# Slot-ordered scratch for the keys and queries of a cross attention, loads behind the row of maxima, and batch 1's keys in the score loop

## What is computed

```python
x = _layernorm(x + _L0_attn_ref(x, ...))
def _L0_xattn_ref(x, cross_input, ...):
    q, k, v = x @ Wq + bq, x @ Wk + bk, x @ Wv + bv          # split in 16 heads
    y = softmax(q k^T * scale, causal) v
    qc, kc, vc = x @ Wcq + bcq, cross_input @ Wck + bck, cross_input @ Wcv + bcv
    y = y + softmax(qc kc^T * scale) vc                       # 256 queries x 1601 keys
    return y @ Wp + bp
x = _layernorm(x + _L0_xattn_ref(x, ctx_512, ...))
```

## Time and profile before

| | before |
|---|---|
| median of 3 runs | 784.41 us |
| lowest and highest | 782.75, 788.08 us |
| profiled execution, device time | 783.82 us |
| its span (first to last instruction) | 781.7 us |
| PE, DVE, ACT, POOL busy | 639.9, 521.7, 428.6, 175.6 us |
| bytes moved by DMA | 62.51 MB in 33067 packets |
| mean granted clock of PE | 0.904 |

### The profile page before, as it was taken

How to read it: one execution, slowest core, us unless ns; L and a number is a source line. 1 busy time by engine, 2 the same in 40 slices (tenths; PEclk the granted TensorE clock), 3 DMA queues, 4 the chain that set the end, 5 groups by cost and what they waited for, 6 DMA issues and landing times. The chain is left out here.

```text
span 781.7 us, 13389 instructions
## 1 busy us (share of the span) xinstructions
PE 639.9 (82%) x5152; PEld 350.8 (45%) x5152; DVE 521.7 (67%) x683; ACT 428.6 (55%) x774; POOL 175.6 (22%) x204
## 2 busy tenths in 40 slices
PE   7988589899999999999968769997304789887996
PEld 5654233333333333333323347883101466655884
DVE  4356979698999999999333458994587444526442
ACT  3555178688888888888860125555630212234223
POOL 6225344246760000000004120000240280004100
PEclk9999779899999999999995669999856879999999
DMA  7045656654341111110020057440000300000000
GB/s 187 1 138 200 196 164 206 208 172 132 105 123 52 49 49 50 49 49 3 4 74 24 1 202 309 140 134 0 0 0 0 149 0 1 1 0 1 1 0 28
DMA packets 33067, 62.51 MB, mean 80 GB/s; under 512 B 6968, under 2 KB 23360, under 8 KB 32496
## 3 DMA queue, kind: packets, MB, share of 16 engines
q1 hardware_dynamic: 26960, 31.84, 13.0%
q0 software_dynamic: 5440, 27.61, 10.2%
q10 hardware_dynamic: 608, 2.25, 1.3%
HBM read 41.46 MB, written 19.77 MB: 78 GB/s over the span
## 5 line engine op out<-in xcount | busy, mean ns | idle before, releaser
L853 ACT ACTIVATE prob<-ps 128x512 f32<-128x512 f32 (+2 forms) x480 | 252.5, 582 | 60.5 <-PE ps L676 53.9
L975 DVE TENSOR_REDUCE pm<-ps 128x2 f32<-128x1024 f32 x192 | 226.2, 1220 | 17.2 <-PE ps L638 15.3
L676 PE MATMUL ps<-qq,kc 50*128 50x256 bf16 (+1 forms) x832 | 136.7, 279 | 8.0 <-DMA qq<-mrow 7.9
L699 PE MATMUL ps<-prob,vst 128*9 128x256 f32 (+1 forms) x1664 | 130.1, 385 | 9.5 <-ACT o_all L841 9.5
L638 PE MATMUL ps<-kc,qq 48*128 48x512 bf16 x384 | 119.9, 401 | 4.8 <-DVE pm L975 3.5
L676 PEld LDWEIGHTS ps<-qq,kc 50*128 50x128 bf16 (+1 forms) x832 | 53.0, 96 | 103.6 <-ACT prob L853 72.7
L1097 POOL TENSOR_TENSOR y<-y 128x256 f32<-128x256 f32 x16 | 11.4, 722 | 193.5 <-issue 178.9
L699 PEld LDWEIGHTS ps<-prob,vst 128*9 128x9 f32 (+1 forms) x1664 | 25.1, 88 | 51.4 <-ACT prob L853 37.7
L982 DVE TENSOR_REDUCE nm<-ps 128x4 f32<-128x512 f32 (+1 forms) x32 | 30.6, 958 | 14.6 <-PE ps L626 14.5
L1778 ACT ACTIVATE prob<-s 128x512 f32<-128x512 f32 (+1 forms) x28 | 15.5, 567 | 45.3 <-PE s L1716 45.3
L638 PEld LDWEIGHTS ps<-kc,qq 48*128 48x128 bf16 x384 | 33.6, 95 | 13.6 <-DVE pm L975 8.9
(11 more groups left out here) (348 smaller groups left out, 1287.1 us busy)
## 6 DMA issues: line engine op xcount, KB each, us to landing
kc<-kc_scr SPq DMA_DIRECT2D x32, 150.1 KB
comb_bc<-comb_scr SPq DMA_DIRECT2D x8, 512.0 KB, 4.6
ctx<-ctx_scr POOLq DMA_DIRECT2D x1, 3204.0 KB, 16.0
kc<-kc_scr SPq DMA_DIRECT2D x32, 100.1 KB
raw<-in_wexp POOLq DMA_DIRECT2D x8, 384.0 KB, 7.8
exp_scr<-raw_high POOLq DMA_DIRECT2D x8, 384.0 KB, 3.5
exp_scr<-raw_low POOLq DMA_DIRECT2D x8, 384.0 KB, 7.0
up_high<-exp_scr SPq DMA_DIRECT2D x8, 256.0 KB, 2.8
```

The source lines that it names most:

```text
L676: last = pe.matmul(bank[0:p, j * TQ:(j + 1) * TQ], kc[s][rows, j, t * 128:t * 128 + p], qq[s][rows, 0, j, :], start=(j == 0), stop=True, s ...
L699: last = pe.matmul(o_ps[32 * hh:32 * hh + VW, kind * TQ + q0:(kind + 1) * TQ], value[:, hh * VW:(hh + 1) * VW], prob[0:k, (NST * n + t) % ...
L853: act.activation(prob[0:p, g % P_RING, 2 * e:2 * e + 2, q0:TQ], s2[0:p, k % S2_RING, 0:2 * w].rearrange("p (i q) -> p i q", i=2), ACT.Exp, ...
L975: dve.tensor_reduce(pm[:, m % 2, c, :, jt], banks, AX.X, ALU.max).then_inc(s1_read, 1)
```

## The change

It has five parts. (a) `kc_scr` and the three other scratches are laid out in slot order, [batch, 64 channels, 6 rows, 2 heads, columns], so that the 48 rows of a head pair lie together; every part is written in as many copies as the slot has: 6 writes for a batch of context keys instead of 3 (twice the bytes), and 6 for each kind of query or own key instead of 3 (the same bytes). (b) A unit is loaded with 2 transfers for the context keys instead of 6, so 8 instead of 12. (c) Batch 0's context keys are written by SP in three slabs (pieces 0, 1, and 2 with 3) as their parts become ready, instead of by POOL at the end; the cast of the masks on POOL comes after piece 1. (d) SP loads unit 1 ahead of the first row of maxima, and then unit m + 2 behind the row of unit m (before: units 1 and 2 ahead, unit m + 3 behind). (e) Batch 1's four key pieces and three value tiles, which stood ahead of the halves, move among the 22 halves; `late_keys` and `late_values` say which half each follows: keys at halves 0 to 7 and 13 to 16, values at 1, 3, 5, 7, 8 to 12, 14, and 16 to 20. The clearing of `o_ps` on DVE moves with them.

```diff
+PART_AT = (1, 2, 0)
-        kc_scr = nc.dram_tensor("kc_scr", [3, NB, 128, TK], BF16).ap()
-        xs_scr = {n: nc.dram_tensor(f"{n}_scr", [NB, 6, 128, TQ], BF16).ap() for n in ("ks", "qs", "qc")}
+        kc_scr = nc.dram_tensor("kc_scr", [NB, 64, 6, 2, TK], BF16).ap()
+        xs_scr = {n: nc.dram_tensor(f"{n}_scr", [NB, 64, 6, 2, TQ], BF16).ap() for n in ("ks", "qs", "qc")}
...
+            FIRST_SLABS = ((0, 0, 512), (1, 512, 512), (3, 1024, TK - 1024))
+            KEYS_OUT = ((first_out, 96 * len(FIRST_SLABS)), (j_out[1], 96), (j_out[0], 96), (j_out[1], 192))
...
-            FIRST_X, SECOND_X, SECOND_KEYS, LATE_KEYS = 4, 7, 10, 14
+            FIRST_X, SECOND_X, LATE_KEYS = 4, 7, 10
...
-            LATE_VALUES = DVE_VALUES + 3
+            late_keys = dict(zip([*range(8), *range(13, 17)], range(LATE_KEYS, len(pieces))))
+            late_values = dict(zip([1, 3, 5, 7, *range(8, 13), 14, *range(16, 21)], range(DVE_VALUES, len(values_order))))
...
                         for e in range(2):
-                            at, row = GROUP * e, 32 * g + 16 * e
-                            for part, r0, copies in ((0, 0, 3), (1, 3, 2), (2, 5, 1)):
-                                src = kc_scr[part, b, row:row + 16, :].rearrange("(c j) t -> c (j t)", j=2)
-                                sp.dma_start(kc[s][at + HD * r0:at + HD * (r0 + copies)],
-                                             src.unsqueeze(0).to_broadcast([copies, HD, 2 * TK])).then_inc(slot_in[s], 16)
+                            row = 16 * g + HD * e
+                            sp.dma_start(kc[s][head_rows(e)], kc_scr[b, row:row + HD].rearrange(
+                                "c r j t -> (c r) (j t)")).then_inc(slot_in[s], 16)
...
-                        if kind == "ks":
-                            for part, r0, copies in ((0, 0, 3), (1, 3, 2), (2, 5, 1)):
...
+                        for r in range(6):
+                            src = xk[:, KPART[r], q] if kind == "ks" else xq[:, PART_AT[QPART[r]], ("qc", "qs").index(kind), q]
+                            sp.dma_start(xs_scr[kind][b, :, r], src).then_inc(x_out[kind][b], 16)
...
-                            src = xs_scr[kind][b, :, row:row + 16, :].rearrange("r (c j) t -> r c (j t)", j=2)
+                            src = xs_scr[kind][b, row:row + HD].rearrange("c r j t -> (c r) (j t)")
...
+                    for j, c0, w in FIRST_SLABS:
+                        for ready, part in (((j_hi, j + 1), hi), ((j_mid, j + 1), mid), (lows(j), low)):
+                            sp.wait_ge(*ready)
+                            for r in range(6):
+                                if (hi, mid, low)[KPART[r]] is part:
+                                    sp.dma_start(kc_scr[0, :, r, :, c0:c0 + w], part[:, 0, c0:c0 + w]).then_inc(first_out, 16)
...
-                    for m in (1, 2):
-                        load_context(m)
+                    def load_unit(n):
+                        if n % NG == 0:
+                            sp.wait_ge(*KEYS_OUT[n // NG])
+                        if n >= SLOTS:
+                            sp.wait_ge(av_done, NST * (n - SLOTS + 1))
+                        load_context(n)
                         for kind in X_KINDS:
-                            load_split(kind, m)
+                            load_split(kind, n)
+
+                    load_unit(1)
                     for m in range(NU):
                         max_rows(m)
-                        n = m + SLOTS - 1
-                        if m < 3:
+                        if m < NB - 1:
                             for kind in X_KINDS:
                                 split_out(kind, m + 1)
-                        if n < NU:
...
+                        if m + 2 < NU:
+                            load_unit(m + 2)
...
-                        for part, src in enumerate((hi, mid, low)):
-                            pool.dma_start(kc_scr[part, b], src[:, b % 2, :]).then_inc(j_out[b % 2], 16)
+                        for r in range(6):
+                            src = (hi, mid, low)[KPART[r]]
+                            pool.dma_start(kc_scr[b, :, r], src[:, b % 2, :]).then_inc(j_out[b % 2], 16)
...
-                        if j in last_piece and is_ctx[j]:
+                        if j in last_piece[1:] and is_ctx[j]:
...
                     for h in range(HALVES + S1_LEAD):
                         half(h)
-                        if LATE_KEYS + h < len(pieces):
-                            keys(LATE_KEYS + h)
-                        if LATE_VALUES + h < len(values_order):
-                            values(LATE_VALUES + h)
+                        if h in late_keys:
+                            keys(late_keys[h])
+                        if h in late_values:
+                            values(late_values[h])
```

More of the change, by code:

```diff
@@ L271, in parts_of @@
                     return [xk[:, part, c0:c0 + w] for part in range(3)]
-                return [xq[:, part, ("qc", "qs").index(kind), c0:c0 + w] for part in (1, 2, 0)]
+                return [xq[:, part, ("qc", "qs").index(kind), c0:c0 + w] for part in PART_AT]
             def wait_parts_left(engine, j):
                 if is_ctx[j] and groups[pieces[j][0]][1] >= 2:
-                    engine.wait_ge(j_out[groups[pieces[j][0]][1] % 2], 16 * 3)
+                    engine.wait_ge(*KEYS_OUT[groups[pieces[j][0]][1] - 2])
             def low_on_dve(j):
@@ L360, in load_split @@
                         if g == 0:
[L361 removed]
+                            sp.wait_ge(x_out[kind][b], 16 * 6)
                         for e in range(2):
[L363 to L365 removed]
+                            row = 16 * g + HD * e
+                            dst = ks[s][head_rows(e)] if kind == "ks" else qq[s][head_rows(e), ("qc", "qs").index(kind)]
+                            src = xs_scr[kind][b, row:row + HD].rearrange("c r j t -> (c r) (j t)")
                             sp.dma_start(dst, src).then_inc(slot_in[s] if kind == "qc" else self_in[s], 16)
@@ L453, in _ @@
                         pool.dma_start(later[n][:], a[n]).then_inc(later_in, 16)
-                    for s in range(2):
-                        pool.wait_ge(j_out[s], 16 * 6)
+                    for b in range(NB):
+                        pool.wait_ge(*KEYS_OUT[b])
                     pool.wait_ge(v_act, len(values_order) - DVE_VALUES)
@@ L616, in _ @@
                         values(5 + i)
-                    for i in range(4):
-                        keys(SECOND_KEYS + i)
-                        if i < 3:
-                            values(DVE_VALUES + i)
                     def add_mask(o, mask, e):
@@ L823, in _ @@
                     high(4)
-                    for j in range(5, SECOND_KEYS):
+                    for j in range(5, LATE_KEYS):
                         middle(j - 1)
                         high(j)
-                    for i in range(4):
-                        middle(SECOND_KEYS + i - 1)
-                        high(SECOND_KEYS + i)
-                        if i < 3:
-                            values(DVE_VALUES + i)
-                    for i in range(len(values_order) - LATE_VALUES):
-                        if LATE_KEYS + i <= len(pieces):
-                            middle(LATE_KEYS + i - 1)
-                        if LATE_KEYS + i < len(pieces):
-                            high(LATE_KEYS + i)
-                        values(LATE_VALUES + i)
+                    for h in range(HALVES + S1_LEAD):
+                        if h == 0:
+                            middle(LATE_KEYS - 1)
+                        if h - 1 in late_keys:
+                            middle(late_keys[h - 1])
+                        if h in late_keys:
+                            high(late_keys[h])
+                        if h in late_values:
+                            values(late_values[h])
                     def copy_out(n):
@@ L964, in _ @@
                         values(5 + i)
-                    for i in range(4):
-                        rest(SECOND_KEYS + i)
                     def reduce_half(m, i):
@@ L1003, in _ @@
                                 row(m - 1)
-                            if m == 0 and LATE_KEYS + i < len(pieces):
-                                rest(LATE_KEYS + i)
+                            if m * HALVES + i in late_keys:
+                                rest(late_keys[m * HALVES + i])
+                            if m * HALVES + i == max(late_values) + 1:
+                                dve.wait_ge(v_act, len(values_order) - DVE_VALUES)
+                                dve.memset(o_ps, 0.0).then_inc(o_zero, 1)
                         combine(m)
-                        if m == 0:
-                            dve.wait_ge(v_act, len(values_order) - DVE_VALUES)
-                            dve.memset(o_ps, 0.0).then_inc(o_zero, 1)
                     row(NU - 1)
```

20 lines of the change are left out of this document (4 added, 16 removed).

## The result

The changed kernel takes 796.82 us (median of 4 runs, 796.11 to 797.77) against 786.25 us (4 runs, 782.75 to 790.75) for the kernel before: 1.013 times as long, interval 1.007 to 1.019. The forecast was 770 us. The profiled execution has 797.43 us, against 783.82.

The account below looks back on a forecast made before the run. PE, busy for 82% of the span, was taken to bound the kernel, with gains only where it waits for transfers. From 783.8 us: -10.0 - 2.7 - 4.6 + 2.8 + 0.5 gives 769.8, stated as 770; range 763 to 781.

Parts of the forecast that it names:

- term 4: Unit 2's load, now behind the row of maxima and 18 writes, lands late for half 30: 2.8 us lost, bounds 0 and 10.
- The lead-in: From half 0 to the first row of maxima: 28.2 us instead of 29.5, ACT's buffer wait gone; bounds 27 and 33.
- Half 0: Start of the first half: at 53.3 instead of 59.82 us, 6.5 us sooner; at 58 with the upper bounds.
- Why the loads land sooner: Unit loads: old ones use 2 or 3 DMA engines, the new 48 rows 16, so a load is spread evenly.
- Term 1: Start of step 0, after the first row of maxima: at about 89.0 instead of 99.00 us, 10.0 us gained.
- term 2: PE's clock at the first steps: four steps at 1.25 instead of 1.94 us, 2.7 us gained; bounds 0 and 2.7.
- term 3: PE's stop at unit 2's step 0: row of maxima issued into an empty queue, 4.6 us gained; bounds 0 and 4.6.
- The forecast for units 3 and 4: Their loads' way from the row of maxima takes 17.1 of a unit's 18.8 us; 0.5 us lost in all.
- A price by bytes: Other pricing of the doubled writes: 2.0 us plus bytes at 436 GB/s; unit 2 in time, 2.8 us less in the sum.
- The second rival: The 18 writes ahead of unit loads cost the loaded 0.94 us each; units 2 to 4 late, 793 us; chance 0.07.
- The last rival: Unit loads land as late as now, the spreading over engines does not come: 12 us slower, 796 us; chance 0.04.
- the first rival: Doubled key writes, at a mean near 200 GB/s, take the gain back at half 13 and units 2 to 4: 779.5 us; chance 0.15.

## Why the prediction was wrong

The step that failed is term 4, the way from a row of maxima to the landing of the next load: the price of a write and the landing were both too small, and a loss put at 3.3 us was 22. The lead-in and the clock gave less than forecast beside it.

*Half 0: right.* The two executions don't start alike; the last value tiles of x are at 49.50 instead of 51.35 us. Counted from them half 0 comes after 2.14 us instead of 8.47, 6.3 us sooner; forecast 6.5. Why the executions start apart isn't shown; the 1.85 us are no part of the forecast.

*Why the loads land sooner: right.* A steady unit load, in windows of the kernel before and of the changed one:

```profile
280.00:282.00 2.00, 2.00 (x40) 0.89 (x37) 2.00 (x3) 1.99 (x5) 0.00 (x0) 1.00 0.26 90
282.00:284.00 2.00, 2.00 (x39) 0.91 (x33) 1.04 (x3) 1.73 (x4) 0.00 (x0) 1.00 0.30 105
```
```profile
284.00:286.00 2.00, 2.00 (x33) 0.70 (x29) 1.98 (x3) 1.70 (x4) 0.00 (x0) 1.00 1.08 212
286.00:288.00 2.00, 2.00 (x34) 0.89 (x31) 2.00 (x3) 1.55 (x4) 0.00 (x0) 1.00 0.98 160
```

A share of 0.2 to 0.3 for ten microseconds (278 to 288) has become one of 1.0 for four (284 to 288), with 0.37 in the window ahead. The packets of SP's queue agree with the rule of the Trainium skill ("DMA: Bandwidth & Descriptors", "Why a DMA increments its semaphore by 16 and not by 1"). The queue rows of the kernel before, of the layout alone, and of the change:

```profile
q1 hardware_dynamic: 26960, 31.84, 13.0%
```
```profile
q1 hardware_dynamic: 28592, 31.85, 16.3%
```
```profile
q1 hardware_dynamic: 31184, 34.31, 17.5%
```

The layout alone has 1632 more, for the same bytes. If each transfer adds one packet for each engine that it uses, and these are 3, 2 and 8 for the old key loads, 6 for the old `qq` and `ks` loads and 16 for the rest, that is 16 units x (8 x 16 - 2 x 13 - 6 x 6) = 1056 plus 36 more writes x 16 = 576: 1632. The change adds 18 slab writes of 64 x 2 rows on SP: 18 x (128 + 16) = 2592, and 31184 - 28592 is 2592. These are sums that fit; no view names the engines of a transfer.

*The lead-in: the term's mechanism right, its size wrong.* ACT's wait of 4.92 us went, as forecast. But the row of maxima came 33.6 us after half 0 (51.64 to 85.27), not 28.2, which is above the upper bound of 33 as well. Two things were missing from the sum. First, POOL issued six key writes instead of three ahead of a low part; DVE's remainder stood for it, 1.74 us, PE was idle for 2.44 us at 70.73, and ran at 1.2 GHz through the next halves, 2.1 to 2.3 us apart instead of 1.26. DVE of the changed kernel:

```profile
68.85 0.69 DVE L891 TENSOR_TENSOR rem<-ps,hi 128x512 f32<-128x512 f32 x1 [1.74 <-POOL low L432]
```

I had counted the writes' bytes and not what stood behind them on POOL. Second, the halves now begin while PE is at half clock. Windows of the changed kernel and of part (d) undone:

```profile
54.00:56.00 2.00, 2.00 (x5) 0.86 (x5) 1.07 (x2) 0.95 (x2) 0.00 (x0) 0.50 0.41 104
```
```profile
54.00:56.00 2.00, 2.00 (x11) 1.15 (x11) 1.82 (x2) 1.24 (x4) 0.39 (x1) 1.00 0.36 100
```

The first three halves with their keys take 8.0 us in the one (51.64 to 59.68) and 4.9 in the other (52.06 to 56.93). Part (d) undone has the same wait for POOL, 1.75 us, and its lead-in still takes only 29.3 us (52.06 to 81.34), about as little as the 28.9 us with POOL's writes later. So POOL's line is only one part of the miss, and the clock of the first halves is as large a one; why it differs between these two kernels, whose lists are the same up to there, isn't shown. **Term 1** thus was 5.6 us (step 0 after 42.0 us, counted from the value tiles, instead of 47.65), not 10.0.

*The clock, term 2: wrong.* Step 0 no longer waits, yet the clock is 0.51 at 96 us. Step 8 is reached 12.0 us after step 0 (103.56), not 10. The 2.7 us never came, and there were fewer to be had: the kernel before took 11.3 us for these eight steps, 1.3 more than eight full ones. PE stood at the first steps for DVE's maxima, 0.4 to 0.9 us each, but that alone doesn't explain the clock: with POOL's writes later it stood 0.47 and 0.94 us in the same places and kept the full clock.

*The stop at unit 2's step 0, term 3: right.* It is gone. Its 4.6 us can't be read in the changed kernel, where unit 2 is late. With the loads first, row 0 to row 4 takes 80.7 us (83.86 to 164.58) against 84.5 before (89.35 to 173.80): 3.7 us for terms 2 and 3 together, of 7.3 forecast.

*Unit 2's load, term 4: this is what turned the sign.* I took 0.49 us for a write, from a transfer of the old form, where the new form takes 0.63 unloaded and 0.68 to 0.90 in place. I took 2 us for `qc` to land, where it took 4.5 to 6.4. The forecast for units 3 and 4, 17.1 of 18.8 us, had thus 3.5 to 4 us too little in the writes and 2.7 to 4.2 in the landing, and a chain that fits into a unit's time became one that doesn't, three times over. A price by bytes, which the prediction gives beside it (12.0 us for the 4.35 MB, unit 2 in time), misses the same thing: the 18 writes took 16.2 us to issue. 2.8 + 0.5 us were forecast; the order cost 22 (796.8 - 774.5).

The second rival, 793 us, had the mechanism and its mark, three waits for the load at steps 8, 23 and 38. I set it at 0.07 because I took the loaded price of rows 5, 0.94, for a full line; the runs show that 0.63 of the new form's 0.68 to 0.90 is issuing. That its time comes within 4 us is partly luck: its writes are dearer than they were, and it kept the 17.3 us of gains, where the kernel with the loads first gained about 11 (ratio 0.986). The last rival, loads that land as late as now, has 796 us and is nearest of all, by coincidence: it puts half 0 at 57.4, which came at 51.64, and the loads land sooner, as shown above. (The prediction's text on the rule says that "the first rival below" would follow if the rule failed; it is this last one.)

*The doubled writes, the first rival,* rested on a rate near 200 GB/s, and that is not what came: batch 1's writes run at 378 and 384 GB/s (66 to 70 us), and in the changed kernel they hold up no buffer. They are not free, though. Out of the way of unit 2's load they took 4.2 us off its wait (7.55 to 3.39), while the time stayed.

What stays open: why the first steps fall to half clock in most versions and not in the two with POOL's writes later, and whether any version is faster than the 774 us of loads first, since the rest lie within the spread of the runs. No run has the loads first and the old lead together, and none has the slot-ordered load without the doubled bytes, so what the doubling costs by itself isn't measured.

## What to carry to other kernels

A chain of issues on one queue between a signal and the load that answers it must fit, with its landing, into the time by which the load runs ahead, here the time of one unit; price each issue by the loaded row, and ask what happens if it is 20% longer, since beyond the edge each unit pays anew, and pays the slow clock on top. Issue first what is due first: here the writes wanted two units later stood ahead of the load wanted next, and one moved block turned 1.3% slower into 1.4% faster. Before giving up lead because the loads have become faster, add up that chain: the shorter lead alone, in the old layout, cost 2.5%.

## What the runs showed of the hardware

A load with its 48 rows in one block brings the DMA share to 1.0 and lands some 2.5 times sooner: `qc` is used 4.5 us after its issue, against 11.2 in the old layout with the same lead. But it is dearer for the engines. Summed over its windows a unit's load kept them busy for 2.9 us before and 5.0 us now, for the same 0.9 MB; SP's queue went from 13.0% to 16.3% of the span with the layout alone and the same bytes. The queue has 1632 packets more, 1056 of them from the loads; at the mean of its packets before (13.0% of 16 x 781.7 us over 26960, 0.06 us each, an estimate) they would make up about a quarter of the 407 us more. What the rest is wasn't tested.

A write of the new form costs SP 0.63 us (3.76/6) and one of the old 0.49 (1.47/3), although the old one moves 64 to 192 KB and the new one 64: in these rows the price goes with the form of the transfer and not with its bytes.
